# A dense graph network on one core: normalisation moved into attention's tail, APPNP's first body moved into the last product of layer 1

## The chip, the cores and the metric

The kernel runs on one core of a Trainium2 chip. The metric is device time in microseconds (us), as the median of three runs. In the text PE is TensorE, DVE is VectorE, ACT is ScalarE, POOL is GpSimd and SP is SyncE, whose queue issues the DMAs spoken of here.

## The reference

A graph of 6250 nodes with 96 features and 100,000 edges goes through four layers. Each layer takes `h = relu(layernorm(x))` and adds its result to x.

```python
h = jnp.maximum(_layernorm(x, axis=-1), 0.0)
x = x + _L0_gnn_ref(h, qW, kW, vW, src, dst)      # attention over the edges, itself h + res
h = jnp.maximum(_layernorm(x, axis=-1), 0.0)
x = x + _L1_gnn_ref(h, src, dst, W, b)            # softmax aggregation: (h + sum(a * m)) @ W + b
h = jnp.maximum(_layernorm(x, axis=-1), 0.0)
x = x + _L2_gnn_ref(h, edge_index)                # APPNP: ten times out = 0.9 * spmm(out) + 0.1 * h
h = jnp.maximum(_layernorm(x, axis=-1), 0.0)
x = x + _L3_gnn_ref(h, edge_index, W1, b1, W2, b2)  # two graph convolutions
...
# layer 1, per destination node and feature
m = relu(feat[src]) + EPS
ex = exp(m - seg_max[dst]);  denom = segment_sum(ex, dst)
msg = segment_sum(ex / denom[dst] * m, dst)
```

## The kernel before, in words

**Tiles and bodies.** The nodes lie in 49 tiles of 128. X (the running x), H (the norm's result) and T hold 49 x 96 floats per partition. Work on them goes in seven bodies of seven tiles (`BODIES` = `RING` = 7, `tiles_of(b)`), so one instruction on a body has 672 elements per partition.

**Attention.** A loop over pairs of tiles builds one-hot matrices from the edge list, gathers keys, values and queries with them on PE, and sums the weighted values. It also builds two dense count matrices in DRAM: `adjacency` (`c_d`), and its transpose `adjacency_t` (`t_d`), which SP writes through transposing DMAs. Each engine runs its own step function `lag` chunks behind the first; the last tile has five chunks (`last_chunks`) and is written out after the loop (`paired`). Attention's result per tile lies in R, whose first 49 tiles are T. Near the end DVE makes `most_all`, the largest count and degree, and `verdict` turns it through a PE transpose into a flag `fits`, which every engine loads before it branches into the dense layers. Nothing of the dense layers is ahead of that branch.

**Layer 1 (`softmax_dense`).** A prelude makes, for each body, X += T, the norm (`Norm.center`, `square`, `variance`, `deviation`, `scale`), exp, and the f16 operand U in high and low halves (384 columns and one of ones). DVE and ACT do it in a pipeline of turns. Then PE multiplies: for output body i and ring slot r it takes 7 x 7 matmuls of 385 columns from the slot into seven PSUM banks. A ring slot holds a block of counts for seven source tiles. Output body i needs U of all seven bodies, slot by slot, so the first output body consumes the prelude as it comes. After a body, ACT copies the low halves out, DVE adds and divides (`inv`, `dn`, T), PE applies the weight matrix in two parts of four and three tiles (`Folded`: transposes L449, products L465, in a bank of its own, called l), DVE adds to X, and the norm for the next layer follows, which ends with ACT writing Ua (`y` in the rows; u_ready). For bodies 0 to 5 these pieces lie between the matmuls of the next body; those of body 6 come after all (`folded.last`).

**APPNP.** Ten steps, each seven bodies of seven banks; bank r of a body takes 49 matmuls of 192 columns (one per source tile) from slot r, loaded from `adjacency_t`. The first bank of a step starts with 42 tiles and waits there for the last seven. ACT and DVE finish each bank (`rows`, `copies`), in loops on every engine. `degree_columns` stands ahead of it on DVE and ACT.

What sets the order is the code as written: each engine runs its queue in order, and semaphores join them.

## Time and profile before

| | us |
|---|---|
| Median of three runs (4059.42 to 4060.96) | 4060.95 |
| Profiled execution, its own time | 4059.11 |
| Its span in the profile | 4057.7 |
| PE busy | 3871.5 (95%) |
| DVE busy | 1833.1 (45%) |
| ACT busy | 1303.2 (32%) |
| POOL busy | 519.8 (13%) |

The profile is of one execution. Its time is 1.4 us above its span, which is what lies outside the span. An engine's share is over all stages; a change in one stage has to be read from that stage's rows.

### The profile page before, as it was taken

How to read it: one execution, taken by the hardware profiler on the slowest of the kernel's cores; microseconds unless marked ns; L12 is line 12 of the kernel's file. 1: busy time of each engine (PE TensorE's matmuls, PEld its weight loads, DVE VectorE, ACT ScalarE, POOL GpSimd, SP SyncE). 2: the span in 40 equal slices, each digit the busy share in tenths (PEclk: the TensorE clock that was granted, in tenths of full speed). 3: DMA queues.
4: the chain of work that ended last, by engine and by line, in shares of the span. 5: the costliest groups of instructions: out<-in, count | busy, mean ns of one | idle time of the engine just before them, and what ended most of it. 6: DMA issues, size and time to landing. Idle time of an engine off the chain costs nothing.

```text
span 4057.7 us, 123846 instructions
## 1 busy us (share of the span) xinstructions
PE 3871.5 (95%) x46211; PEld 3663.5 (90%) x46211; DVE 1833.1 (45%) x4350; ACT 1303.2 (32%) x3904; POOL 519.8 (13%) x708
## 2 busy tenths in 40 slices
PE   3779999999979998999999999999999998999998
PEld 2669999999956665999999999999999998999998
DVE  8989999999983224222222222222222222331221
ACT  1238878788871101222222222222222221111110
POOL 1005555555520000000000000000000000000000
PEclk9989999999989999999999999999999999999999
DMA  1029999999963332566656556656655665666674
GB/s 40 3 52 236 229 228 234 233 227 228 235 190 109 110 109 84 197 203 204 204 203 203 202 202 202 202 203 203 203 203 203 204 202 178 204 218 210 210 220 142
DMA packets 437963, 747.69 MB, mean 184 GB/s; under 512 B 197295, under 2 KB 330543, under 8 KB 437804
## 3 DMA queue, kind: packets, MB, share of 16 engines
q1 hardware_dynamic: 432808, 744.50, 60.9%
q8 instruction: 123, 2.02, 0.2%
q10 hardware_dynamic: 4996, 0.88, 0.1%
q14 instruction: 36, 0.29, 0.0%
HBM read 621.82 MB, written 83.32 MB: 174 GB/s over the span
## 4 chain that ended last, share of the span: by engine, by line
PE 91%; DVE 6%; ACT 1%; issue 1%; DMA 1%; ACTq 0%; SPq 0%; DVEq 0%
PE sum L1651 49%; PE sum L1344 19%; PE pk L1114 10%; PE pr L1137 7%; PE pq L1126 3%; PE pc L1150 2%; DVE onerank L759 2%; PE l L465 1%; DVE bt L731 1%; DVE prodb L748 1%; DVE vals L741 0%; PE l L449 0%; DMA X<-in_x_dram 0%; DVE sameb L736 0%; DVE kv L593 0%
## 5 line engine op out<-in xcount | busy, mean ns | idle before, releaser
L1651 PE MATMUL sum<-y,ring 128*128 128x192 f16 x12005 | 995.1, 247 | 4.0 <-ACT y L1500 4.0
L1651 PEld LDWEIGHTS sum<-y,ring 128*128 128x128 fp8e4 x12005 | 993.8, 98 | 4.6 <-issue 4.2
L1651 PE MATMUL sum<-u2b,ring 128*128 128x192 f16 x12005 | 993.0, 247 | 0.0
L1651 PEld LDWEIGHTS sum<-u2b,ring 128*128 128x128 fp8e4 x12005 | 992.1, 98 | 0.2
L1660 DVE TENSOR_TENSOR z<-lo,sum 128x96 f32<-128x96 f32 x441 | 112.3, 255 | 1006.7 <-ACT lo L1675 1006.1
L1114 PE MATMUL pk<-kv,hT 128*128 128x192 f16 x4900 | 487.1, 247 | 11.2 <-DVE hT L1008 9.6
L1344 PE MATMUL sum<-u,ring 128*128 128x385 f16 x2401 | 402.7, 328 | 22.2 <-ACT u L1468 22.2
L1114 PEld LDWEIGHTS pk<-kv,hT 128*128 128x128 f16 x4900 | 406.0, 99 | 18.2 <-DVE hT L1008 9.5
L1344 PEld LDWEIGHTS sum<-u,ring 128*128 128x128 fp8e4 x2401 | 235.7, 98 | 182.5 <-issue 24.6
L1675 ACT ACTIVATE lo<-sum 128x96 f32<-128x96 f32 x441 | 110.3, 250 | 668.5 <-PE sum L1651 668.5
L1137 PE MATMUL pr<-wv,hs_wide 128*128 128x101 f32 x2450 | 321.3, 278 | 1.2 <-POOL wv L1071 1.2
L1137 PEld LDWEIGHTS pr<-wv,hs_wide 128*128 128x128 f32 x2450 | 292.9, 192 | 1.5 <-POOL wv L1071 1.5
L1196 ACT ACTIVATE kvs<-pk 128x384 f32<-128x384 f32 x735 | 277.7, 441 | 25.6 <-PE pk L1114 21.6
L1071 POOL TENSOR_TENSOR wv<-kvs,wv 128x480 f32<-128x480 f32 x245 | 255.2, 1041 | 107.4 <-ACT wv L1176 107.4
L1066 POOL TENSOR_SCALAR sc<-sc,bound 128x20 f32<-128x20 f32 x245 | 188.7, 770 | 477.6 <-DVE sc L992 477.1
L1344 PE MATMUL sum<-u2b,ring 128*128 128x192 f16 x2401 | 203.0, 246 | 0.7 <-ACT u2b L1817 0.7
L1344 PE MATMUL sum<-y,ring 128*128 128x192 f16 x2401 | 202.2, 246 | 0.0
L1344 PEld LDWEIGHTS sum<-u2b,ring 128*128 128x128 fp8e4 x2401 | 199.1, 98 | 1.1 <-ACT u2b L1817 1.0
L1344 PEld LDWEIGHTS sum<-y,ring 128*128 128x128 fp8e4 x2401 | 199.0, 98 | 0.1
L1169 ACT ACTIVATE row<-pc 128x512 uint16<-128x512 f32 (+1 forms) x343 | 187.1, 549 | 1.0 <-PE pc L1150 0.2
L1186 ACT ACTIVATE hs_wide<-hs 128x640 f32<-128x640 bf16 x245 | 179.0, 731 | 0.0
L1663 DVE SCALAR_TENSOR_TENSOR uf<-z,col_g,H 128x96 f32<-128x96 f32 x441 | 140.6, 319 | 81.6 <-DVE z L1660 81.6
(237 smaller groups left out, 3412.6 us busy)
## 6 DMA issues: line engine op xcount, KB each, us to landing
ring<-adjacency_t SPq DMA_DIRECT2D x490, 800.0 KB, 4.3
ring<-adjacency SPq DMA_DIRECT2D x147, 896.0 KB, 4.8
rows<-slot_rows_d SPq DMA_DIRECT2D x249, 320.0 KB, 4.2
adjacency<-row SPq DMA_DIRECT2D x49, 800.0 KB, 4.3
adjacency_t<-col SPq DMA_DIRECT2D x49, 800.0 KB, 4.8
col<-row SPq DMA_TRANSPOSE x245, 4.5
out_dram<-X SPq DMA_DIRECT2D x6, 336.0 KB
ed<-in_dst_dram ACTq DMA_DIRECT2D x25, 18.0 KB, 1.7
```

Source lines behind the costliest of these rows:

```text
L1066: pool.tensor_scalar(sc[i][:], sc[i][:], k.bound[:, 0:1], k.bound[:, 1:2], ALU.min, ALU.max).then_inc(k.clipped.sem, 1)
L1071: pool.tensor_tensor(wv[i][:, :, 0:D].rearrange("p g (h d) -> p g h d", d=DH), kv[i][:, :, D:2 * D].rearrange("p g (h d) -> p g h d", d=DH ...
L1114: t = pe.matmul(pk[n][:, place:place + 2 * D], hT[i][:, 1 + m, g, :], k.kv[:, 2 * (g0 + g) + m, part, :], start=m == part == 0, stop=m == ...
L1126: t = pe.matmul(pq[i][:, g * D:(g + 1) * D], hT[i][:, 0, g, :], q2[b][:, part, :], start=part == 0, stop=part == 1)
L1137: t = pe.matmul(pr[:, 0:AV], hs_wide[e % HOMES][:, g, :], wv[i][:, g, :], start=g0 + g == 0, stop=g0 + g == GROUPS - 1)
L1169: a.activation(flat(row[b][:, g:g + count, :]), pc[u % 2][:, 0:count * P], ACT.Copy, accum_out=rowsum[:, bass.ds(X * (2 * UP) + u, 1)]).th ...
L1186: a.activation(flat(hs_wide[e % HOMES][:]), hs[e % 2][:].rearrange("p g a t -> p (g a t)"), ACT.Copy).then_inc(k.wide.sem, 1)
L1196: a.activation(flat(kv[i][:, 2 * n:2 * n + count, :]), pk[n][:, 0:count * 2 * D], ACT.Copy).then_inc(k.kv_out.sem, 1)
L1344: t = pe.matmul(self.ps[j][:, 0:self.cols], w[:, q, (j + odd) // 2, :, (j + odd) % 2], U[:, r * RING + q, 0:self.cols], start=r == q == 0, ...
L1651: m = pe.matmul(ps[r][:, 0:2 * D], w[:, t // 2, :, t % 2], n["this"][:, t, 0:2 * D], start=t == 0, stop=t == TILES - 1)
L1660: v.tensor_tensor(z[:, j, :], lo[:, j, :], ps[j][:, 0:D], ALU.add).then_inc(k.free.sem, 1)
L1663: v.scalar_tensor_tensor(uf[j][:], z[:, j, :], k.g[:, tile], flat(k.H[:, tile, :]), ALU.mult, ALU.add).then_inc(k.uf.sem, 1)
```

## The change

Four things are done.

1. In attention's tail, DVE does X += T and `center` for body 0 and ACT squares it (`first_norm`, at step `last_chunks + 1`); after the last operations on `most`, DVE does `variance` and `scale`, and ACT the root and the exp, all ahead of the verdict. SP loads ring slot 0 for layer 1 there, ahead of the last three transposes. For this the ring is seven buffers, of which the first lives from the start.
2. X += R of bodies 1 to 6 goes from DVE, where it stood in the prelude, to POOL, in one row after attention's last result. The column `odeg` is copied one step earlier on POOL, and one small operation of the verdict goes into the tail.
3. The prelude of layer 1 is written in another order: body 0's operand alone first, then body by body.
4. The last product of layer 1 goes straight on into APPNP's first body: six banks over 42 tiles, with the four pieces of body 6 between them, then the last seven tiles of these six banks, then bank 6. `adjacency_t` is loaded for it as the slots come free. DVE's chain of layer 1 is cut in two, four tiles and three. The loop over APPNP's steps is regrouped, with body 0 left out of the first step on PE and SP.

```diff
@@ sync_step
+        if chunks == last_chunks and c == SP_LAG:
+            Blocks.load(k, 0, 0)
@@ denominate / normalize
+        pool.tensor_copy(k.odeg[:, bass.ds(2 * X + b, 1)], sums[b][:, AV - 1:AV]).then_inc(k.degreed.sem, 1)
...
-        pool.tensor_copy(k.odeg[:, bass.ds(2 * X + b, 1)], sums[b][:, AV - 1:AV])
@@ paired
+            if meanwhile and c == last_chunks + 1:
+                meanwhile()
@@ vector (attention)
-        paired(v, vector_step)
+        paired(v, vector_step, meanwhile=first_norm)
...
+        norm.variance(0)
+        norm.scale(0)
+    def first_norm():
+        t = tiles_of(0)
+        v.wait_ge(k.normed.sem, k.normed.at((RING - 1) // 2, (RING - 1) % 2))
+        v.tensor_tensor(k.X[:, t, :], k.X[:, t, :], k.R[:, t, :], ALU.add).then_inc(k.added.sem, 1)
+        v.wait_ge(k.added.sem, k.added.at(1))
+        norm.center(0)
+    def gpsimd():
+        paired(pool, gpsimd_step)
+        pool.wait_ge(k.normed.sem, k.normed.at(PAIRS - 1, last_tiles - 1))
+        for b in range(1, BODIES):
+            t = tiles_of(b)
+            pool.tensor_tensor(k.X[:, t, :], k.X[:, t, :], k.R[:, t, :], ALU.add).then_inc(k.added2.sem, 1)
+    def scalar():
+        paired(a, scalar_step, meanwhile=lambda: norm.square(0))
+        norm.deviation(0)
+        a.wait_ge(k.ln_h.sem, k.ln_h.at(1))
+        a.activation(k.T[:, tiles_of(0), :], k.H[:, tiles_of(0), :], ACT.Exp).then_inc(k.exps.sem, 1)
@@ softmax_dense, vector
+            product(0)
+            remainders(0)
+            center(1)
+            norm.variance(1)
+            for b in range(1, BODIES):
+                if b + 1 < BODIES:
+                    center(b + 1)
+                norm.scale(b)
+                if b + 1 < BODIES:
+                    norm.variance(b + 1)
+                product(b)
+                remainders(b)
...
+                for h, (j0, j1) in enumerate(Folded.PARTS):
+                    for j in range(j0, j1):
...
+                    v.reciprocal(inverse, inverse).then_inc(k.inv.sem, 1)
@@ softmax_dense, tensor
-            blocks.tensor([k.lo2], folded)
+            for i in range(BODIES):
+                blocks.products(i, [k.lo2], folded)
+            first_products()
+            there = TILES - RING
+            pe.wait_ge(k.u_ready.sem, k.u_ready.at(there))
+            for r in range(RING - 1):
+                begin_panel(r)
+                for half in range(2):
+                    panel(r, range(half * there // 2, (half + 1) * there // 2))
+                    folded.piece(BODIES - 1, 2 * r + half - 2)
+            pe.wait_ge(k.u_ready.sem, k.u_ready.at(TILES))
+            for r in range(RING - 1):
+                panel(r, range(there, TILES))
+            begin_panel(RING - 1)
+            panel(RING - 1, range(TILES))
```

DVE's queue in attention's tail, before, from the last score sum on; `highest`, `filled` and `fits` are the verdict's.

```order
L992 TENSOR_REDUCE sc<-qk 128x20 [waits at_exped,at_scored]
L1044 RECIPROCAL rden<-rden 128x4 [waits at_denom]
L1242 CAST bits<-rowsum 128x343 [waits at_out_c]
L1244 TENSOR_REDUCE most<-odeg 128x1 [waits at_normed]
L1246 TENSOR_SCALAR bits<-bits 128x343 [waits most_s]
L1247 TENSOR_SCALAR most<-most 128x1
L1249 TENSOR_REDUCE most<-bits 128x1 [waits most_s]
L1251 TENSOR_TENSOR most_all<-most 128x1 [waits most_s]
L1271 TENSOR_REDUCE highest<-pf 1x1 [waits most_s,at_normed,most_ps,at_col_out1,at_col_out0]
L1273 TENSOR_SCALAR highest<-highest 1x1 [waits verdict]
```

The same place in the change:

```order
L1267 TENSOR_TENSOR X<-X,T 128x672 [waits at_normed]
L278 TENSOR_REDUCE col<-X 128x7 [waits added]
L280 TENSOR_SCALAR col<-col 128x7 [waits ln_sum]
L282 TENSOR_TENSOR H<-X,col 128x672 [waits ln_mean]
L1047 RECIPROCAL rden<-rden 128x4 [waits at_denom]
...
L1259 TENSOR_TENSOR most_all<-most 128x1 [waits most_s]
L292 TENSOR_REDUCE col<-T 128x7 [waits ln_sq]
L294 TENSOR_SCALAR col<-col 128x7 [waits ln_var]
L304 RECIPROCAL col<-col 128x7 [waits ln_std]
L306 SCALAR_TENSOR_TENSOR H<-H,col 128x672 [waits ln_rstd]
L1303 TENSOR_REDUCE highest<-pf 1x1 [waits most_s,at_normed,most_ps,at_col_out1,at_col_out0]
```

Four operations stand ahead of the last reciprocal of attention now, and four between `most_all` and the verdict's first.

ACT's queue from the last exp of attention to the first part of U, in the change (`wv` is that exp, `sums` attention's last sums):

```order
L1180 ACTIVATE wv<-sc,score_unit 128x5x4 [waits at_summed,at_clipped]
L287 ACTIVATE T<-H 128x672 [waits ln_cen]
L1207 ACTIVATE sums<-pr 128x101 [waits at_normed,at_summed]
L299 ACT_TABLE_LOAD
L299 ACTIVATE col<-col 128x7 [waits ln_vare]
L1282 ACT_TABLE_LOAD
L1282 ACTIVATE T<-H 128x672 [waits ln_h]
L1310 TENSOR_LOAD fits [waits most_s,at_normed,verdict,at_col_out1,at_col_out0]
```

The square stands ahead of the copy of attention's last sums; root, exp and their two table loads stand ahead of the verdict. Before, they came after it.

PE's queue at the end of layer 1, before, from the last slot's last banks on (l is the bank of the weight matrix's pieces):

```order
L1344 MATMUL sum_6<-u,ring 128x385 x7
L449 MATMUL l<-ident,T 96x128 [waits lin_out,agg]
L449 MATMUL l<-ident,T 96x128 x3
L465 MATMUL l<-wl,aT 128x96 [waits lin_copied]
L465 MATMUL l<-wl,aT 128x96 x3
L449 MATMUL l<-ident,T 96x128 [waits lin_out,agg]
L449 MATMUL l<-ident,T 96x128 x2
L465 MATMUL l<-wl,aT 128x96 [waits lin_copied]
L465 MATMUL l<-wl,aT 128x96 x2
```

The same place in the change:

```order
L1558 MATMUL sum<-y,ring 128x192 [waits ring0,free,u_ready]
L1558 MATMUL sum<-y,ring 128x192 x41
L1558 MATMUL sum<-y,ring 128x192 [waits ring1,free]
L1558 MATMUL sum<-y,ring 128x192 x41
L449 MATMUL l<-ident,T 96x128 [waits lin_out,agg]
L449 MATMUL l<-ident,T 96x128 x3
L1558 MATMUL sum<-y,ring 128x192 [waits ring2,free]
L1558 MATMUL sum<-y,ring 128x192 x20
L465 MATMUL l<-wl,aT 128x96 [waits lin_copied]
L465 MATMUL l<-wl,aT 128x96 x3
L1558 MATMUL sum<-y,ring 128x192 x21
L449 MATMUL l<-ident,T 96x128 [waits lin_out,agg]
```

84 matmuls of APPNP's first body are ahead of the first piece, 21 between each two pieces, and 105 more follow the last one ahead of the wait for the last seven tiles.

## Rows read from the trace of the kernel before

**Rows 1.** The page: chain that ended last, shares of the span by line.

```profile
PE sum L1651 49%; PE sum L1344 19%; PE pk L1114 10%; PE pr L1137 7%; PE pq L1126 3%; PE pc L1150 2%; DVE onerank L759 2%; PE l L465 1%; DVE bt L731 1%; DVE prodb L748 1%; DVE vals L741 0%; PE l L449 0%; DMA X<-in_x_dram 0%; DVE sameb L736 0%; DVE kv L593 0%
```

**Rows 2.** Chain in order of time, longest pieces: start us, us, what.

```profile
1183.97 74.78 PE sum L1344 x441
...
1285.32 32.41 PE sum L1344 x196
...
1623.06 1809.40 PE sum L1651 x21910
```

**Rows 3.** Chain, around the verdict.

```profile
1157.78 3.33 DMA adjacency_t<-col
...
1162.54 0.16 DVE fits L1277
...
1163.46 0.95 DVE X L1413
```

**Rows 4.** Chain, from layer 1's last product to APPNP.

```profile
1580.19 16.22 PE sum L1344 x98
...
1599.03 4.36 DVE inv L1434
...
1605.20 0.87 DVE T L1440
...
1613.70 0.47 DVE X L1391
```

**Rows 5.** Timeline of the tail: start us, us, engine, line, operation, [idle before <-releaser].

```profile
1151.63 0.65 DVE L992 TENSOR_REDUCE sc<-qk 128x20 f32<-128x480 f32 x1
...
1152.50 0.35 POOL L1066 TENSOR_SCALAR sc<-sc,bound 128x20 f32<-128x20 f32 x1 [0.46 <-DVE sc L992]
...
1155.73 0.26 ACT L1203 ACTIVATE sums<-pr 128x101 f32<-128x101 f32 x1 [2.53 <-PE pr L1137]
...
1157.46 0.34 POOL L1089 TENSOR_TENSOR T<-sums,rden 128x96 f32<-128x96 f32 x1
```

**Rows 6.** Timeline of the kernel's start, DVE beside POOL.

```profile
23.58 1.60 POOL L212 TENSOR_TENSOR X<-X,H 128x672 f32<-128x672 f32 x1 [21.17 <-DVE H L306]
24.29 0.91 DVE L294 TENSOR_SCALAR col<-col 128x7 f32<-128x7 f32 x1
...
49.86 1.60 POOL L212 TENSOR_TENSOR X<-X,H 128x672 f32<-128x672 f32 x1 [1.87 <-DVE H L306]
49.87 1.90 DVE L510 TENSOR_TENSOR wq_squares<-wq 96x288 f32<-96x288 f32 x1
```

**Rows 7.** DVE's groups, 1152 to 1240: count | busy us, mean ns | idle before.

```profile
L306 DVE SCALAR_TENSOR_TENSOR H<-H,col 128x672 f32<-128x672 f32 x7 | 6.0, 858 | 0.2
...
L294 DVE TENSOR_SCALAR col<-col 128x7 f32<-128x7 f32 x7 | 1.2, 172 | 0.2
```

**Rows 8.** Timeline, ACT in the prelude of layer 1.

```profile
1171.04 0.76 ACT L287 ACTIVATE T<-H 128x672 f32<-128x672 f32 x1 [2.35 <-DVE H L282]
...
1171.83 1.28 ACT L1476 ACT_TABLE_LOAD   x1
...
1173.12 0.76 ACT L1476 ACTIVATE T<-H 128x672 f32<-128x672 f32 x1
```

**Rows 9.** Timeline, ACT's copy of a body's seventh bank (layer 1's first, APPNP's first).

```profile
1242.64 0.33 ACT L1489 ACTIVATE lo<-sum 128x192 f32<-128x192 f32 x1 [0.83 <-PE sum L1344]
...
1649.75 0.25 ACT L1675 ACTIVATE lo<-sum 128x96 f32<-128x96 f32 x1 [1.52 <-PE sum L1651]
```

**Rows 10.** Chain, two pieces of the weight matrix within a later body.

```profile
1553.62 0.44 PE l L449 x4
...
1562.16 0.86 PE l L465 x8
```

**Rows 11.** Windows: stretch, length, PE, PEld, DVE, ACT, POOL busy, PEclk, DMA share, GB/s.

```profile
1606.00:1616.00 10.00, 7.89 (x37) 6.64 (x38) 2.92 (x7) 1.08 (x2) 0.00 (x0) 0.50 0.01 6
...
1170.00:1175.00 5.00, 0.00 (x0) 0.00 (x0) 4.79 (x10) 3.88 (x5) 0.00 (x0) 0.50 1.09 386
```

More of the change, by code:

```diff
@@ L1352, in products, with sync @@
                 folded.piece(i - 1, r)
-    def sync(self, ended=None):
+    def sync(self, ended=None, early=0):
         n = len(self.U) * BODIES
         for i in range(n):
-            self.loads(i)
+            self.loads(i, 0 if i else early)
             if ended and i >= 2:
@@ L1421, in vector @@
                 v.wait_ge(k.agg.sem, k.agg.at(i))
-                for j in range(RING):
-                    t = RING * i + j
-                    v.wait_ge(k.low.sem, k.low.at(t + 1))
-                    v.tensor_tensor(dn[:, j, :, :], lo[:, j, :, :], halves(ps[j])[:, :, 0, :], ALU.add).then_inc(k.sums.sem, 1)
-                    v.tensor_scalar(k.ideg[:, t:t + 1], ps[j][:, cols - 1:cols], UNIT, None, ALU.mult).then_inc(k.free.sem, 1)
-                tiles = tiles_of(i)
-                v.wait_ge(k.free.sem, k.free.at(RING * i + RING))
@@ L1638, in loads @@
             k.settle(sp)
[L1639 removed]
+            sp.dma_start(k.ring[r][:, 0:WIDE], k.t_d[RING * n["body"] + r, :, :]).then_inc(k.ring_in[r].sem, 16)
     def products(n):
@@ L1683, in numbers, with bodies @@
     def numbers(eng):
-        def bodies(step, U, Un):
+        def bodies(step, U, Un, first=0):
             if eng is pe:
@@ L1688, in bodies @@
                 k.settle(pe)
-            with eng.Fori(0, BODIES) as i:
+            with eng.Fori(first, BODIES) as i:
                 yield {"step": step, "body": i, "at": step * BODIES + i, "this": U, "next": Un}
+        yield from bodies(0, Ua, Ub, 1 if eng in (pe, sp) else 0)
         with eng.Fori(0, last // 2) as s:
-            yield from bodies(2 * s, Ua, Ub)
             yield from bodies(2 * s + 1, Ub, Ua)
-        yield from bodies(last - 1, Ua, Ub)
+            yield from bodies(2 * s + 2, Ua, Ub)
     def last_numbers():
@@ L1846, in dense_layers @@
     with ExitStack() as ctx:
-        k.ring = k.buf(ctx, "ring", [P, RING, SLOT], U8)
+        k.ring += [k.buf(ctx, f"ring_{r}", [P, SLOT], U8) for r in range(1, RING)]
         Y = k.buf(ctx, "y1", [P, TILES, D], F32)
         Ua = Y[:].bitcast(F16)
-        with ExitStack() as banks:
-            softmax_dense(k, [k.bank(banks, f"sum1_{j}") for j in range(RING)], k.bank(banks, "l1"), Y, Ua)
-        appnp_and_convolutions(k, ctx, [k.bank(ctx, f"sum2_{j}") for j in range(RING)], k.bank(ctx, "l3"), Ua, out)
+        ps, bank = [k.bank(ctx, f"sum_{j}") for j in range(RING)], k.bank(ctx, "l")
+        softmax_dense(k, ps, bank, Y, Ua)
+        appnp_and_convolutions(k, ctx, ps, bank, Ua, out)
 class Edges:
```

180 lines of the change are left out of this document (101 added, 79 removed).

## The prediction, as it was put on record

> **What bounds the kernel now.** The page's chain first: it is PE almost throughout, most of it APPNP's matmuls [rows 1]. So the change can only win where PE stands. The chain in order of time shows two such places: PE ends attention just ahead of ACT's copy at 1155.73 [rows 5] and starts layer 1 at 1183.97 [rows 2], and it ends layer 1's last product at 1580.19 + 16.22 = 1596.41 [rows 4] and starts APPNP for good at 1623.06 [rows 2], after 42 early matmuls. Then I read both places in the chain and the timeline, for what ends each wait. A matmul of 385 columns costs 32.41 / 196 = 0.1654 us, a body's slot of 49 costs 8.10, one of 192 columns 1809.40 / 21910 = 0.0826, a bank of 49 costs 4.05 [rows 2].
>
> **First place, the tail, without contention.** Before, the verdict's last operation ends at 1162.70, DVE's first of layer 1 starts at 1163.46 [rows 3], and the prelude lasts until 1183.97. After, body 0's norm and exp are there. What is left is three DVE operations on a body (product, two remainders, 0.86 each, as L306 [rows 7]) and one ACT copy (0.76, as the exp [rows 8]). With one small verdict operation less (0.17 [rows 7]), PE would start at 1163.3 + 3 x 0.87 + 0.9 = 1166.8.
>
> **What POOL takes back.** DVE stands beside POOL's X += H on a body, 1.60 us [rows 6]: a tensor_scalar that takes 0.17 alone [rows 7] took 0.91, until POOL ended, and a small tensor_tensor started at 49.87 ended at 51.77, just after POOL's 51.46. So DVE's operations with two SBUF inputs, and its tensor_scalar, wait for POOL's current operation. The change puts six such POOL operations, 9.6 us, right behind attention's last result, beside the DVE operations that lead to the verdict.
>
> When do they start? The last score sum ends at 1152.28; DVE's X += T takes until 1153.15, and POOL's clip, before at 1152.50, waits for it: 0.7 late, and exp, weighting and sums with it. DVE's reduction ends at 1154.0, its tensor_scalar waits for POOL's weighting, the centred H is there at 1156.0 (0.86 each), ACT's square at 1156.8. The copy of the last sums stands behind it: 1156.8 for 1155.73 [rows 5]. POOL's last result, before at 1157.80 [rows 5], comes at 1158.85, and its six additions start there.
>
> If both engines take turns, the maximum on DVE comes at 1160.7 (if single-column tensor_scalars don't need the port) or 1162.4 (if they do); then the variance (reduction 0.86, tensor_scalar behind an addition), root and reciprocal 0.5, scale behind an addition: 1164.9 or 1166.6. The verdict's maximum 0.3, comparison, and `fits` behind one or two more: 1166.65 or 1170.1, for 1162.70. From there 0.75 to the branch, and three DVE operations, two or none of them behind an addition: PE starts at 1173.25 or 1174.35. I take 1173.8. Each addition can block once, so both ends lie close. If DVE got no turn until POOL is through (1168.5), what needs the port after the maximum follows from there: 1176.
>
> Behind this cover the rest of the tail costs nothing. The exp's two table loads (1.28 each [rows 8]) and the exp end at 1165.7 or 1167.4, ahead of `fits`. SP's load of slot 0 (0.92 MB, 2.4 us at 386 GB/s [rows 11]) stands ahead of three transposes and the stores that end at 1161.11 [rows 3]; even 2.4 us late, 1163.5, PE's transpose of the maximum is done before DVE gets to its result. Without POOL's contention those 2.4 us would be the loss.
>
> The Trainium skill, SBUF — State Buffer, § Who interferes with whom, says that the pair is an exclusive lock, held by whichever starts first for the whole instruction, by a DVE operation with two SBUF inputs against a POOL operation that reads SBUF, and that a tensor_reduce never contends. By this rule, the trace agrees with it (0.91 for 0.17).
>
> **The prelude, body by body.** PE wants a body's U every 8.10 us. In the new order the engines hand each body back and forth: from the second remainder of body b-1, DVE centres b+1 (1.95), ACT squares (0.76), loads a table (1.28), takes the exp (0.76) and its copy (0.77) of b, loads the root's table (1.28), takes the root (0.2, half of it beside the next) and the second copy (0.75), and DVE takes the second remainder (0.86); with gaps of 0.02 and the root's wait 8.68. Body 1 has no head start: its U comes 12.3 after PE's start (centre 1.95, square and table 2.1, root; centre of 2 and square 2.4; table, exp, copy, table, root, copy 5.0; remainder and copy 1.7, less the 0.9 between remainder and PE's start). PE's first slot ends at 8.1 + 1.95 for the low clock: the first body of before ended at 1242.62 [rows 9], 58.65 after its start for 343 x 0.1654 = 56.7. So PE waits 2.3 for body 1 and 0.58 for each of 2 to 5; body 5 is ready at 12.3 + 4 x 8.68 = 47.0, body 6 needs two things less and is in time. The first body ends 47.0 + 2 x 8.10 = 63.2 after PE's start: 1237.0, for 1242.62. **Gain 5.6.** X += T of six bodies off DVE (0.86 each) helps only in that DVE isn't the longer of the two. The later slots are 0.92 MB each, landed at 2.4 us apart, ahead of 8.10.
>
> The Trainium skill, ScalarE: Activation LUTs, § What ACT_TABLE_LOAD costs, has every switch at about 2.66 us, with a drain of 1.38 beside the load. Here the square ends at 1171.80, the load starts at 1171.83 and the exp at 1173.12: 1.28 and no drain [rows 8]. By the page a body would take 8.68 + 2.76 = 11.4 and this place would lose about 8 us; by the row it gains 5.6.
>
> **Second place: into APPNP.** Slots and U are there: each slot is free 8.1 us after the one before, long ago, and Ua of bodies 0 to 5 since the piece of body 5. PE runs on at 1596.43 with 84 matmuls, 6.9 us, to 1603.4. DVE's chain: four tiles are summed at 1593.8 (three banks of 1.16 ahead of PE's end, and 0.9 for ACT's copy and DVE's sum) and cost 4/7 of a chain in which the reciprocal is 4.36 and five others 0.87 [rows 4, 7]: to 1599.1; then three tiles' sums (1.3) and 3/7: T at 1604.7 for 1606.07 [rows 4]. Banks 4 to 6 are freed at 1599.5, 1599.9 and 1600.4; in the six bodies where PE wants them again, it does so 4 x 1.16, 5 x 1.16 and 6 x 1.16 after the body's end, 1601.0 and later: covered by 1.5 us. PE waits 1.3 for T. Pieces at full clock are 0.44 and 0.86 for four tiles [rows 10], three quarters for three. With the 21 matmuls (1.73) that stand between them: transposes to 1605.3, 21 to 1607.0, products to 1608.0, DVE 0.56, 21 to 1609.7, transposes 1610.1, 21 to 1611.8, products to 1612.6, DVE's last addition to 1613.1, for 1614.17 [rows 4]. From there to PE's start on the last seven tiles it is 1623.06 - 1614.17 = 8.89 as before: 1622.0. PE has 105 matmuls, 8.7, until 1621.2, waits 0.8, and takes 42 + 49 in 7.5: APPNP's first body ends at 1629.5. Before, 1649.7 [rows 9]: 301 x 0.0826 = 24.9 after 1623.06, and 1.8 left over, which the new order doesn't repeat if the clock stays up. **Gain 20.2.** Rows and loads of the next body start as banks end and have 4.05 each for 2.6 of work on ACT and DVE, so the crowd of six early banks is gone within the next body.
>
> **Sum.** 5.6 + 20.2 = 25.8 off the profiled execution's 4059.11. The median lies 1.84 above it: 4060.95 - 25.8 = **4035 us**.
>
> **Rivals.**
> *Low clock across the second place.* Before, the granted clock was 0.50 from 1606 to 1616 although PE worked there [rows 11], after 9.7 us of idling. If the 1.3 us of waiting brings it about, at half speed the four pieces take 2.3 longer and the three times 21 matmuls between them at most 5.2. I take 6 of these 7.5, since the fall needn't cover all: gain 14, total 20: 4041. For it: small matmuls and waits. Against: PE is busy nine tenths of the place. 0.17.
> *No turns for DVE in the tail*, or a body cycle longer by half a microsecond: the first place gives 2 or nothing: 4038 to 4041. 0.16.
> *POOL hardly in the way*: the operations that stand beside its additions don't need the port, as the trace shows only two kinds [rows 6]. Then PE starts at 1166.8 plus up to 2.4 for the slot's load, gain 5 to 7 more: 4029. Against: both kinds are the ones used here. 0.10.
> *Slower, by layer 1's banks.* The split chain sits ahead of the sums of banks 4 to 6. If it takes longer than worked out by more than the cover of 1.5 us, PE stalls at bank 4 of each of six bodies. To turn 25.8 us into a loss of 8, it must stall 5.6 a body: the four tiles' part would take 12.4 us instead of 5.3. 0.04.
> *The change doesn't do what it says in the second place*: APPNP's early banks wait for a slot or a bank, so that PE idles as before. Against: slots come free 8.1 us apart. 5.6 us of gain, 4055. 0.04.
> *Table switches stand still for longer than the load*, say another 1.28 each, now that ACT's chain is the one that PE waits for. Body 1 would come 3 x 1.28 later, each further body 2.56: the first place loses 8, the total gain is 12, 4049. The exp right behind its load speaks against it [rows 8]. 0.01.
> The forecast has 0.48.
>
> **Range.** 4029 to 4043 takes in the forecast and the first three rivals, 0.91, with 2 us for the estimates in them. A measurement of this kernel tells a difference from 0.2%, 8.1 us. Faster than that: all cases but two, 0.92; within it (the second place not doing what it says) 0.04; slower 0.04.
>
> **What would show it.** POOL has six operations of about 1.6 from 1158.9 on, and DVE's tensor_scalar and two-input ones between `most_all` and the verdict last until one of them ends. `fits` ends 4 to 7 us later than before, PE starts layer 1 near 1174, waits 2 to 3 us at its second slot and about 0.6 at the next four. T of body 6 comes 8.3 after the last product's end, PE idles under 3 us from there to the end of APPNP's first body, at a clock of 1.00, and from then on everything is as before. The prediction is wrong if POOL and DVE run side by side, if the clock falls in the second place, or if a later body of layer 1 is longer than 343 x 0.1654 + 2.3 for its four pieces = 59.0.

## The result, and the profile after

Four runs of the changed kernel gave a median of 4033.39 us (4032.60 to 4033.83), four of the kernel before 4060.62 (4059.42 to 4060.96): 27.2 us less, a ratio of 0.9934 with a 95% interval of 0.9923 to 0.9946. 4035 had been forecast. The profiled execution has a span of 4032.1 us.

In the page after, the chain by line still is TensorE's [rows 1], and a line of APPNP's early matmuls (L1558) is new in it.

The first place, in the timeline after. These rows answer to [rows 5] (last score sum), [rows 3] (`fits`) and [rows 2] (TensorE's start at 1183.97):

```profile
1152.43 0.65 DVE L995 TENSOR_REDUCE sc<-qk 128x20 f32<-128x480 f32 x1
...
1160.08 10.62 POOL L1276 TENSOR_TENSOR X<-X,T 128x672 f32<-128x672 f32 x6
...
1160.36 0.15 DVE L1257 TENSOR_SCALAR most<-most 128x1 f32<-128x1 f32 x1
...
1163.78 1.74 DVE L306 SCALAR_TENSOR_TENSOR H<-H,col 128x672 f32<-128x672 f32 x1
...
1165.92 1.06 DVE L1307 TENSOR_TENSOR fits<-filled,highest 1x1 int32<-1x1 f32 x1
...
1167.75 1.50 DVE L1496 SCALAR_TENSOR_TENSOR y<-H,T 128x672 f32<-128x672 f32 x1 [0.77 <-DVE fits L1307]
...
1169.17 2.25 DVE L1502 TENSOR_TENSOR T<-T,u 128x672 f32<-128x672 f32 x1
1171.35 0.85 DVE L1504 TENSOR_TENSOR y<-y,u 128x672 f32<-128x672 f32 x1
...
1173.09 9.63 PE L1379 MATMUL sum<-u,ring 128*128 128x385 f16 x49 [8.14 <-ACT u L1521]
1185.39 34.23 PE L1379 MATMUL sum<-u,ring 128*128 128x385 f16 x196 [2.67 <-ACT u L1521]
1219.82 30.43 PE L1379 MATMUL sum<-u,ring 128*128 128x385 f16 x183 [0.19 <-ACT u L1521]
```

While GpSimd adds (1160.08 to 1170.70), H takes 1.74 us for its 0.86 [rows 7], T takes 2.25, and `fits`, one element, 1.06. The single-column tensor_scalar at 1160.36 takes 0.15 in the same stretch, and the row at 1171.35, right after GpSimd is through, 0.85. TensorE starts at 1173.09 and ends its first body at 1219.82 + 2 x 8.10 = 1236.02, for 1242.62 before.

One thing in this profile was in no forecast. TensorE's last ten matmuls of attention stand ahead of the copy of the last sums, and so ahead of GpSimd's additions. In the timeline after:

```profile
1155.56 2.46 PE L1141 MATMUL pr<-wv,hs_wide 128*128 128x101 f32 x10 [1.31 <-POOL wv L1074]
```

and in that of place1_only (below), which has the same tail:

```profile
1155.49 1.36 PE L1141 MATMUL pr<-wv,hs_wide 128*128 128x101 f32 x10 [1.31 <-POOL wv L1074]
```

The wait ahead of them is the same 1.31 us (0.88 before). From 1156 to 1158 the granted clock is 0.50 in the one and 1.00 in the other.

The second place, in the chain after (start us, us, what). It answers to [rows 4]:

```profile
1597.32 0.47 DVE T L1475
...
1597.83 0.64 PE l L449 x4
1598.47 1.73 PE sum L1558 x21
1600.20 0.89 PE l L465 x8
...
1605.60 0.47 DVE X L1428
...
1622.55 2.48 PE sum L1731 x30
```

and two rows of its windows, after:

```profile
1600.00:1616.00 16.00, 15.35 (x181) 15.12 (x179) 8.09 (x16) 3.62 (x8) 0.00 (x0) 1.00 0.01 3
...
1616.00:1632.00 16.00, 16.00 (x197) 16.00 (x195) 6.05 (x23) 4.34 (x18) 0.00 (x0) 1.00 0.95 382
```

Layer 1's last product ends at 1590.03, T is there 7.8 us later and TensorE is through with APPNP's first body 32.5 us later, at 1622.55; before it was 53.3 us. The granted clock is 1.00 (2.4 GHz) in the whole place, where before it was 0.50 [rows 11].

### The profile page after: what moved, and what is told of

It reads as the page before. It is cut to its first block, busy times and chain, and to the rows that moved or that the text cites. A ratio compares the mean times of both kernels' runs of the same rounds, so it can differ in the third digit from the quotient of the medians.

```text
span 4032.1 us, 123897 instructions
## 1 busy us (share of the span) xinstructions
PE 3868.6 (96%) x46211; PEld 3661.2 (91%) x46211; DVE 1835.6 (46%) x4386; ACT 1303.0 (32%) x3904; POOL 526.1 (13%) x714
## 3 DMA queue, kind: packets, MB, share of 16 engines
q8 instruction: 126, 2.06, 0.2%
## 4 chain that ended last, share of the span: by engine, by line
PE 90%; DVE 6%; ACT 1%; issue 1%; DMA 1%; SPq 0%; ACTq 0%; DVEq 0%
PE sum L1731 48%; PE sum L1379 18%; PE pk L1118 10%; PE pr L1141 7%; PE pq L1130 3%; PE pc L1154 2%; DVE onerank L759 2%; PE l L465 1%; DVE bt L731 1%; DVE prodb L748 1%; DVE vals L741 0%; PE l L449 0%; DMA X<-in_x_dram 0%; PE sum L1558 0%; DVE sameb L736 0%
## 5 line engine op out<-in xcount | busy, mean ns | idle before, releaser
L1731 PE MATMUL sum<-y,ring 128*128 128x192 f16 x11662 | 962.9, 246 | 0.0
L1731 PEld LDWEIGHTS sum<-y,ring 128*128 128x128 fp8e4 x11662 | 962.2, 98 | 0.0
L1379 PEld LDWEIGHTS sum<-u,ring 128*128 128x128 fp8e4 x2401 | 236.0, 98 | 172.7 <-issue 11.9
L1379 PE MATMUL sum<-y,ring 128*128 128x192 f16 x2401 | 202.2, 246 | 0.0
L1379 PEld LDWEIGHTS sum<-y,ring 128*128 128x128 fp8e4 x2401 | 199.0, 98 | 0.1
```

What stands on the lines that cost most here:

```text
L1379: t = pe.matmul(self.ps[j][:, 0:self.cols], w[:, q, (j + odd) // 2, :, (j + odd) % 2], U[:, r * RING + q, 0:self.cols], start=r == q == 0, ...
L1731: m = pe.matmul(ps[r][:, 0:2 * D], w[:, t // 2, :, t % 2], n["this"][:, t, 0:2 * D], start=t == 0, stop=t == TILES - 1)
```

## The experiments

Eleven kernels ran, in three groups that each had runs of the kernel before beside them. The table gives medians; "gain" is that of the kernel before in the same group less this one. The kernel before itself moved by up to 1.6 us between groups (4060.62, 4060.01, 4059.22, 4059.01), so a difference of under 1.5 us between two gains is read from stages of the trace and not from the table. Seven are the changed kernel with one edit; place1_only and place2_only undo one half of it, and combined and combined_slot have several edits.

| kernel | median us | before beside it | gain |
|---|---|---|---|
| the changed kernel | 4033.39 | 4060.62 | 27.2 |
| place1_only | 4053.21 | 4060.01 | 6.8 |
| place2_only | 4038.63 | 4060.01 | 21.4 |
| pieces_first | 4046.05 | 4060.01 | 14.0 |
| no_split | 4035.36 | 4060.01 | 24.7 |
| late_slot | 4032.06 | 4059.22 | 27.2 |
| dve_adds | 4035.15 | 4059.22 | 24.1 |
| paced_adds | 4033.39 | 4059.22 | 25.8 |
| dev_last | 4029.97 | 4059.22 | 29.3 |
| squares_early | 4018.67 | 4059.01 | 40.3 |
| combined | 4013.77 | 4059.01 | 45.2 |
| combined_slot | 4012.76 | 4059.01 | 46.3 |

One more thing has to be known before stages are compared. Attention's last score sum starts at 1152.43 in the changed kernel and at 1151.63 before [rows 5]. The difference grows steadily through attention's loop. In the timeline of DVE, the same two score sums of the loop, one from its middle and one from its end, for the changed kernel:

```profile
595.32 0.64 DVE L995 TENSOR_REDUCE sc<-qk 128x20 f32<-128x480 f32 x1
...
1137.03 0.64 DVE L995 TENSOR_REDUCE sc<-qk 128x20 f32<-128x480 f32 x1
```

and for place2_only, which has attention as before:

```profile
595.10 0.64 DVE L993 TENSOR_REDUCE sc<-qk 128x20 f32<-128x480 f32 x1
...
1136.20 0.64 DVE L993 TENSOR_REDUCE sc<-qk 128x20 f32<-128x480 f32 x1
```

541.71 us lie between them for 541.10; the ten others with the changed tail have 541.7 to 542.0, and the kernel before 541.11. That is the second half of the loop only. From the tenth score sum (322.04 after, 322.19 before) to the one at 1137.03 it is 814.99 for 814.04, so the loop is 1.0 us longer. The only edit within the loop is GpSimd's copy of the degrees, which now stands between the denominator and the wait for DVE's inverse. That this copy is what costs the 1.0 us was not tried by itself. In the eleven kernels with the changed tail the last sum starts anywhere from 1151.67 to 1152.90, so in the first place I count from that start: TensorE's first matmul of layer 1 stands 20.66 behind it in the changed kernel.

In four kernels that leave the first place untouched (place1_only, pieces_first, no_split, squares_early) it stands 19.72 behind it. There the last ten matmuls of attention take 1.36 and not 2.46, and GpSimd's additions start 6.71 behind the last score sum and not 7.65. So 0.94 of the 20.66 us are the low clock ahead of the additions, in the one execution that was profiled.

### The two places apart

place1_only undoes the second place, place2_only the first (tail, verdict and prelude as before).

```diff
-            for i in range(BODIES):
-                blocks.products(i, [k.lo2], folded)
-            first_products()
+            blocks.tensor([k.lo2], folded)
```

> The second half of the change is undone (APPNP's first body runs after layer 1's last product, DVE's chain is whole), the tail and the prelude stay as changed. Theory, that the two places add up and share no resource: layer 1's first body still ends at 1236.0 and its last product at 1590.1, and the time is the time before less 6.4, so 4054.2 (4053 to 4055.5). Rival, that the places lean on each other (the earlier prelude is worth less, or more, without the second): a gain of 4 or less, or 9 or more, so over 4056.5 or under 4052.

> The tail, the verdict and the prelude are as before, only the second place is changed. Theory of two places that add up: layer 1 as before (its first body ends at about 1242.6, its last product at about 1596.4), and the end of APPNP's first body 32.5 after that last product, so the time before less 20.8, 4039.8 (4038.8 to 4041). Rival: a part of the 20.8 comes from the first place, then the first body ends more than 34 after the last product and the time is over 4041.5.

The diff shows the main lines of place1_only; place2_only takes back the whole of the tail and the prelude. Measured: 6.8 and 21.4, ratios 0.9984 (0.9974 to 0.9993) and 0.9950 (0.9933 to 0.9966). Together 28.2, for 27.2 of both: the places add up. place1_only's 4053.21 lies in its range, place2_only's 4038.63 is 0.2 under its own. In place2_only, TensorE's rows show the prelude of before (start at 1184.00), and the chain shows APPNP's first body 32.5 us behind the last product, which ends at 1596.4, as in the changed kernel:

```profile
1628.87 11.14 PE sum L1700 x135
```

### The order of the second place

pieces_first puts the four pieces of the last linear ahead of APPNP's panels in TensorE's queue.

```diff
             there = TILES - RING
+            folded.last()
...
                 for half in range(2):
                     panel(r, range(half * there // 2, (half + 1) * there // 2))
-                    folded.piece(BODIES - 1, 2 * r + half - 2)
```

> The four pieces of the last linear (two of transposes, two of products) stand in TensorE's queue before APPNP's first panels and not between them; nothing else is changed. Theory, that the 84 matmuls of two panels and a half fill waits for DVE and ACT that are there anyway: with the pieces first, TensorE stands idle while T is made and copied, the panels begin only behind the last piece, and APPNP's first body ends later by about what those panels take that no longer fit, at most the 10.7 that 126 matmuls of 7.1 us for 84 give, less what still fits under the norm behind the last piece; I take 3 to 10.7, with 4033.4 + 7 = 4040 as middle. Rival, that the interleaving is worth nothing because all of the panels fit under DVE's chain behind the last piece: same within 1 us.

no_split lets DVE work on seven tiles at once.

```diff
-                for h, (j0, j1) in enumerate(Folded.PARTS):
+                for h, (j0, j1) in enumerate(((0, RING),)):
```

> DVE's chain of layer 1 works on all seven tiles at once again, as before the change; APPNP's first body still begins in layer 1's last product. Theory, that the split lets the first four tiles' transposes and copy run beside the chain of the last three: T is finished earlier without the split (one chain and not two), the transposes and copy of the first four tiles come later, net the first body ends later by 1 to 3, time about 4035.3. Rival, that the ready semaphore is raised only after both parts and so the split costs its six more instructions: the unsplit one is faster by 1 to 2, about 4032.

pieces_first lost 12.7 us by the medians and 13.2 by the gains, more than the 10.7 I had given as the most. TensorE's rows in its timeline:

```profile
1597.34 1.09 PE L449 MATMUL l<-ident,T 128*96 128x128 f32 x4 [7.80 <-DVE T L1475]
1599.11 2.02 PE L465 MATMUL l<-wl,aT 97*128 97x96 f32 x8 [0.68 <-ACT aT L458]
1601.87 0.84 PE L449 MATMUL l<-ident,T 128*96 128x128 f32 x3 [0.74 <-DVE X L1428]
```

It waits 7.80 for T, then 0.68 and 0.74, and its pieces take twice the 0.64 and 0.89 of the changed kernel: the granted clock was 0.50 from 1592 to 1608. All 343 matmuls of the body come behind the last piece, 30.20 us from 1604.89, and the body ends 45.6 us after layer 1's last product and not 32.5. I had counted 126 matmuls that no longer fit in front. The two chains give the 13.1 us in three parts. The 84 matmuls that ran under the wait for T now run behind it: 84 x 0.0826 = 6.9. The pieces take 5.6 us for 2.5 and the 343 matmuls 30.2 for 28.3, at the low clock: 4.9, which I had left out. TensorE waits 1.95 between the pieces for ACT and DVE, where the changed kernel waits 0.65 for the last copy: 1.3. The 3 x 21 matmuls between the pieces cover only those waits; their own time is on the chain in either order.

no_split lost 2.0 (2.6 by the gains). T comes 9.7 us after the last product (ended at 1588.34, T at 1598.02), 1.9 later than with the split. My median of 4035.3 was met, but not by its theory, which had T earlier without the split and nothing of the clock. The body ends 35.95 after the product, 3.4 later. The other 1.5 stands in TensorE's rows of the timeline:

```profile
1598.07 1.09 PE L449 MATMUL l<-ident,T 128*96 128x128 f32 x4 [2.79 <-DVE T L1475]
1598.95 3.00 PE L1558 MATMUL sum<-y,ring 128*128 128x192 f16 x21
```

and in its windows:

```profile
1596.00:1600.00 4.00, 1.93 (x11) 1.79 (x12) 2.05 (x4) 0.59 (x1) 0.00 (x0) 0.72 0.00 0
```

After a wait of 2.79 the four transposes take 1.09 for 0.64 and the 21 matmuls behind them 2.79 in the chain for 1.73, and the granted clock is 0.72 in that window. In the changed kernel the wait there is 0.87 and the clock stays at 1.00. So the rival of a low clock in the second place was real: in the profile without the split it is there. Counted from the last score sum, no_split's first place is 0.9 shorter than that of the changed kernel (no low clock in attention's end), so 3.4 less 0.9 stands beside the 2.6.

### Who lengthens DVE's operations, and what that costs

dve_adds takes the additions of bodies 1 to 6 off GpSimd; paced_adds leaves two behind attention and hands out the other four, one in each body.

```diff
+            pool = k.pool
+            for b in range(3, BODIES):
+                t = tiles_of(b)
+                pool.wait_ge(k.res2.sem, k.res2.at(b - 2))
+                pool.tensor_tensor(k.X[:, t, :], k.X[:, t, :], k.T[:, t, :], ALU.add).then_inc(k.added2.sem, 1)
```

> The six additions of bodies 1 to 6 are on DVE again, one before each body's mean, and GpSimd does none. Theory, that GpSimd's additions lengthened DVE's operations between 1160 and 1171 by taking the port: H L306 is back from 1.74 to 0.86, fits from 1.06 to about 0.1 or 0.2, y from 1.50 to 0.86, T from 2.25 to 0.86, so TensorE's first body begins near 1169.8 and not 1173.1; then body 1 comes 0.9 later behind its own addition. Layer 1's first body ends 1 to 3 earlier, and the time is about 4031.5. Rival, that the lengthening is not due to GpSimd (a wait inside the instruction): the same durations stay, and the time is 0.9 or more slower for the additions on DVE.

> GpSimd adds bodies 1 and 2 behind attention as now, and each of bodies 3 to 6 only when the remainders of body b - 3 are taken (one addition of 1.6 to 1.8 in each body). Theory, that only the overlap of the additions with the first body's chain costs: additions end near 1163.6, H, fits, y and T of the first body take 0.9 or less each, TensorE's first matmul comes near 1169.9, a gain of 3.1 kept until the end, since the later additions fall where DVE waits for ACT: 4030.3. Rival, that the additions cost the same wherever they stand: each later body is lengthened by 0.7, the gain is under 1.

DVE's and TensorE's rows in the timeline of dve_adds:

```profile
1161.70 0.86 DVE L306 SCALAR_TENSOR_TENSOR H<-H,col 128x672 f32<-128x672 f32 x1
1166.08 0.15 DVE L1303 TENSOR_TENSOR fits<-filled,highest 1x1 int32<-1x1 f32 x1
1166.99 0.94 DVE L1493 SCALAR_TENSOR_TENSOR y<-H,T 128x672 f32<-128x672 f32 x1 [0.77 <-DVE fits L1303]
1167.84 0.85 DVE L1499 TENSOR_TENSOR T<-T,u 128x672 f32<-128x672 f32 x1
...
1170.52 10.12 PE L1375 MATMUL sum<-u,ring 128*128 128x385 f16 x49 [5.07 <-ACT u L1518]
1184.61 18.02 PE L1375 MATMUL sum<-u,ring 128*128 128x385 f16 x98 [3.97 <-ACT u L1518]
...
1213.11 8.27 PE L1375 MATMUL sum<-u,ring 128*128 128x385 f16 x49 [1.23 <-ACT u L1518]
1222.62 27.62 PE L1375 MATMUL sum<-u,ring 128*128 128x385 f16 x166 [1.24 <-ACT u L1518]
```

Every length is back (0.86, 0.15, 0.94, 0.85), and TensorE starts 17.62 behind the last score sum and not 20.66. Of these 3.0 us, 0.94 are the low clock in the changed kernel's profile; against the four kernels at 19.72 it is 2.1, and that GpSimd's additions cost this much of the start is shown. It isn't more because the last transfer of adjacency_t holds the verdict here: it lands 11.9 behind the last score sum, and `highest` follows it by 0.8. But the body cycle is now 1222.62 - 1213.11 = 9.5, for 8.60 in the changed kernel. TensorE waits 3.97 for body 1 and 1.24 at the last two; the last wait ends 2.3 later than in the changed kernel, counted from the last score sum. My 4031.5 had priced one addition of 0.9 on the path, where each body has one.

paced_adds starts TensorE at 17.55, and then shows:

```profile
1169.28 10.90 PE L1379 MATMUL sum<-u,ring 128*128 128x385 f16 x49 [5.07 <-ACT u L1521]
1182.32 8.27 PE L1379 MATMUL sum<-u,ring 128*128 128x385 f16 x49 [2.15 <-ACT u L1521]
1191.65 8.27 PE L1379 MATMUL sum<-u,ring 128*128 128x385 f16 x49 [1.06 <-ACT u L1521]
```

The cycle is 9.35, longer by 0.75. Of 3.1 us at the start 0.1 is left at TensorE's last wait (67.25 behind the last score sum for 67.39), and the median is the same 4033.39. Against the four kernels at 19.72, whose last wait ends 66.45 behind the sum, it is 0.8 worse. My theory fell and its rival held: spread over the bodies of this chain, which goes back and forth between DVE and ACT, each addition costs nearly what it costs on DVE (0.75 for 0.9).

The Trainium skill, SBUF — State Buffer, § Who interferes with whom, has the DVE operations with two SBUF inputs and the GpSimd ones that read SBUF exclude each other for a whole instruction and leaves the reduction alone. These runs agree: 0.86 for 1.74 with the additions gone, and a variance reduction of 0.84 at 1161.62 in the middle of them.

### Slot 0 of the ring

```diff
-        if chunks == last_chunks and c == SP_LAG:
-            Blocks.load(k, 0, 0)
...
-        scalar(), vector(), scalar_sums(), tensor(), blocks.sync(early=1), first_loads()
+        scalar(), vector(), scalar_sums(), tensor(), blocks.sync(), first_loads()
```

> Slot 0 of the ring is loaded behind the verdict again, and not in attention's tail. Theory, that the early load only fills a place where nothing waits for it: the last adjacency_t transfer lands about 3 earlier (near 1161.1 and not 1164.3), but the verdict's last product is held by DVE's H anyway and moves by less than 0.4; slot 0 then lands about 4.6 after its issue, near 1172.6, just before TensorE's first operand at 1173.1. Time within 0.5 of the changed kernel. Rival one, that the three crowded transfers of the tail hold up the verdict: faster by 1 or more. Rival two, that seven loads issued together bring slot 0 later than 1173.1: TensorE's first matmul waits for the ring, slower by 1 to 4.

The gain is the same 27.2 (its median is 1.3 under that of the changed kernel, and the kernel before in its group is 1.4 lower too). The last transfer starts at 1158.91 instead of 1161.00 and lands 9.55 behind the last score sum, for 11.89, and nothing comes of it. DVE's rows of late_slot show why:

```profile
1163.65 1.73 DVE L306 SCALAR_TENSOR_TENSOR H<-H,col 128x672 f32<-128x672 f32 x1
1165.31 0.27 DVE L1301 TENSOR_REDUCE highest<-pf 1x1 f32<-1x128 f32 x1
...
1165.80 1.07 DVE L1305 TENSOR_TENSOR fits<-filled,highest 1x1 int32<-1x1 f32 x1
```

The verdict's maximum stands behind H on DVE, which GpSimd holds up, whether the transfer lands at 1162.2 or at 1164.3. The early load is worth nothing and costs nothing, as long as that cover lasts. In dve_adds, where it doesn't, TensorE starts 17.62 behind the last sum, held by this transfer.

### ACT's root behind both low halves

```diff
-                if 1 <= b < BODIES - 1:
-                    norm.deviation(b + 1)
...
                 if b == 0:
                     norm.square(1)
+                if b < BODIES - 1:
                     norm.deviation(b + 1)
```

> ACT takes the root for body b + 1 (and loads the table of the root) behind both low halves of body b, not between its first and its second copy. Theory from the rows: TensorE waits 2.67 at 1185.4 for body 1's last ACT copy, which stands behind that table load of 1.28; from there on it has hardly any wait (196 matmuls in 34.2). So body 1's copy comes 1.3 to 1.5 earlier, and nothing is gained behind it: 4033.4 - 1.4 = 4032.0. Rival, that the body cycle of 8.6 on ACT sets the pace of all the bodies: with the cycle at 8.1 or less a gain of 3 or more, 4030 or less.

3.4 us less than the changed kernel by the medians, 2.1 by the gains; TensorE's stage gives 3.5. TensorE's rows in the timeline, and ACT's loads of the root's table:

```profile
1173.02 9.91 PE L1379 MATMUL sum<-u,ring 128*128 128x385 f16 x49 [8.38 <-ACT u L1519]
...
1184.00 1.28 ACT L299 ACT_TABLE_LOAD   x1
1184.04 64.98 PE L1379 MATMUL sum<-u,ring 128*128 128x385 f16 x392 [1.11 <-ACT u L1519]
...
1191.63 1.28 ACT L299 ACT_TABLE_LOAD   x1
```

Body 1's copy comes 1.35 earlier (1.5 counted from the last score sum), as expected, but that is not all. ACT's cycle is 1191.63 - 1184.00 = 7.63, for 8.60, so that now TensorE's 8.10 sets the pace: four times 0.5 more. So the rival that I had put beside my theory held. I had read the unbroken row of 196 matmuls in 34.23 us (after, at 1185.39) as TensorE working without a wait. 196 x 0.1654 is 32.4. A window of the changed kernel:

```profile
1186.00:1190.00 4.00, 4.00 (x16) 1.95 (x14) 3.00 (x6) 3.51 (x4) 0.00 (x0) 0.57 0.26 93
```

The slower matmuls filled the time in which others of these kernels show a wait of 0.33 in each body (place1_only, pieces_first and late_slot, whose TensorE rows stand 8.60 apart). The low clock cost nothing there, because ACT's chain ended last either way: from body 1's copy to the last wait it is 34.43 us in the changed kernel and 34.43 in place1_only, whose clock stays at 1.00.

### The squares of the weights

Both traces show TensorE waiting 10.8 us in APPNP's last step for a product of DVE's that nothing keeps from being made earlier. In the timeline before:

```profile
3443.26 0.74 PE L1595 MATMUL l<-w_squares,ones 97*128 97x96 f32 x2 [10.81 <-DVE w_squares L1590]
```

```diff
     def last_rows():
+        unit.squares()
...
-            if b == 0:
-                unit.squares()
```

> DVE squares the weights of the first convolution before the rows of APPNP's last step, and no longer behind body 0's norm; otherwise the changed kernel. Theory from the row PE l <- DVE w_squares 10.8 of the trace after (it stands in the trace of before too): TensorE waits there for nothing but this product, and what it does next has been ready for long, so the time falls by the whole wait, to 4033.4 - 10.8 = 4022.6 (4021.5 to 4024), and a little more if the granted clock after the wait was below full. Rival: behind the wait TensorE meets DVE's and ACT's rows of body 0 anyway (free banks, the lo copies), then less than half of it is gained, 4028 or more.

4018.67, 14.7 less than the changed kernel by the medians (13.1 by the gains). The changed kernel, TensorE's wait in the timeline and a stretch of the windows:

```profile
3416.11 0.74 PE L1676 MATMUL l<-w_squares,ones 97*128 97x96 f32 x2 [10.82 <-DVE w_squares L1671]
```

```profile
3410.00:3420.00 10.00, 3.89 (x23) 3.70 (x24) 4.02 (x8) 2.50 (x4) 0.00 (x0) 0.50 0.01 2
```

and squares_early, the same stretch:

```profile
3410.00:3420.00 10.00, 10.00 (x124) 10.00 (x122) 5.43 (x12) 2.28 (x7) 0.00 (x0) 1.00 0.68 226
```

The wait is gone, and so is the half clock behind it: the next 2058 matmuls take 169.79 us for 172.30. The stage from the end of the panels before to layer 3 is 13.8 shorter: 10.8 of wait and 3.0 of clock. The time is 2.8 under the range I had given: I had the second part as "a little more". The 0.9 between 13.8 and 14.7 is the first place, whose profile has no low clock in attention's end here.

### Together

combined has dev_last, paced_adds and squares_early; combined_slot has slot 0's load behind attention's last transfer as well.

```diff
-        if chunks == last_chunks and c == SP_LAG:
-            Blocks.load(k, 0, 0)
...
     vector(), gpsimd(), paired(pe, tensor_step), scalar(), paired(sp, sync_step, SP_LAG)
+    Blocks.load(k, 0, 0)
```

> Three edits on the changed kernel: ACT's root behind both low halves, GpSimd's additions two behind attention and four paced, the squares of the weights early. The first alone made ACT's cycle 7.64 against TensorE's 8.10, so that there is 0.46 of room in each body; the paced additions alone lengthened the cycle from 8.61 to 9.35 but began TensorE 3.1 earlier. Theory that the two fit together (the 0.75 of an addition goes mostly into that room, since it delays a mean that is not what ACT waits for): body 1's copy 2.1 earlier than with the late root alone and TensorE without a wait behind it, so 4030.0 - 2.1 - 10.8 = 4017.1 (4015.5 to 4018.5). Rival, that the additions cost 0.7 in each later body here too: the cycle is 8.3 to 8.4, of the 2.1 about 1 is left or nothing, 4018.3 to 4019.5.

> As the one before, and slot 0 of the ring is loaded behind the last adjacency_t transfer instead of ahead of the last two transfers of attention. Theory: the last transfer lands about 3 earlier relative to attention's last sum (9.6 behind it and not 11.9 to 12.0), and with DVE's H no longer held up by GpSimd the verdict then comes 1.5 earlier; slot 0 lands before the verdict's branch, and TensorE's first matmul is 15.9 behind the last sum instead of 17.5. All later work moves with it: the combined time less 1.6, 4015.5. Rival one: body 1 and TensorE's own work bind, and of 1.6 nothing is left (within 0.5 of the combined one). Rival two: slot 0's transfer, issued 7 to 10 later, collides with the other six and TensorE starts later than 17.5: slower by 0.5 to 2.

combined: 4013.77, ratio to before 0.9887 (0.9870 to 0.9903). TensorE's rows:

```profile
1171.03 10.67 PE L1379 MATMUL sum<-u,ring 128*128 128x385 f16 x49 [5.07 <-ACT u L1519]
1182.80 64.98 PE L1379 MATMUL sum<-u,ring 128*128 128x385 f16 x392 [1.09 <-ACT u L1519]
```

No wait behind body 1, with an addition in each body: the cycle (GpSimd's additions stand 8.06 apart) now has the room for it. Body 1's copy is 1.5 earlier than in dev_last, counted from the last score sum, of 2.1 expected. The time is 3.3 under the expected 4017.1 and 1.7 under its range; squares_early alone had been 3.9 better than expected.

combined_slot: 4012.76 (4012.30 to 4013.69), ratio 0.9886 (0.9869 to 0.9902). Its chain around the verdict:

```profile
1158.22 4.38 DMA adjacency_t<-col
...
1163.85 0.16 DVE fits L1306
...
1164.77 0.94 DVE y L1495
```

The last transfer takes 4.38 for 3.33, with slot 0 behind it; TensorE starts 16.31 behind the last score sum, for 18.21 in combined, so the first place gives 1.9. By the medians it is 1.0, and the ranges of the two kernels' runs overlap: shown in the stage, not in the time. It is the fastest of all and beats the changed kernel by 20.6 us by the medians, the kernel before by 46.3.

## Why the prediction was right

**The sum.** Forecast 5.6 and 20.2; the stages of the profile show 6.6 and 20.8, and the two kernels with one place each 6.8 and 21.4. 6.6 + 20.8 = 27.4 stands beside the 27.2 measured; 4035 was 1.6 too high. That each part comes so near is in part luck, as the first place shows.

**The first place.** The mechanism held as put: GpSimd's additions lengthen DVE's two-input operations and its tensor_scalar on seven columns (0.77 at 1162.49, for 0.17 [rows 7]), not the reductions. Of the two ends for single-column tensor_scalars the lower one is right (0.15 and 0.14 in the middle of the additions). TensorE's start at 1173.1 lies just under the forecast's 1173.25 to 1174.35. That is nearer than the working deserves. The last score sum came 0.8 later than I had it: attention's loop, where I had costed the moved copy of the degrees at nothing, is 1.0 longer. And 0.94 is the low clock of attention's last ten matmuls, which I hadn't thought of; I had looked for a low clock in the second place only. Against these two stands a chain from the last score sum to the start that I had worked out too long: 21.6 at its lower end (1173.25 - 1151.63) for the 19.72 of the four kernels without the low clock. That DVE wins turns is in the trace after: H ends at 1165.52 and `fits` at 1166.98, with GpSimd adding until 1170.70. The rival that GpSimd is hardly in the way is refuted by dve_adds, by 2.1 to 3.0 us. The prediction set 0.91 for 0.17 beside the rule on two-input operations, but that row is a tensor_scalar's; the pair of rows that bears the rule out is H's 1.74 for 0.86. The prelude behind the start took 62.9 for 63.2, with 2.67 of wait for body 1 (2.3 forecast) and a cycle of 8.60 (8.68). Of the 1.0 us between 5.6 and 6.6, 0.7 is the start and 0.3 the stretch behind it.

**The additions off DVE.** I had valued them only as keeping DVE from being the longer of the two engines. dve_adds shows more: with an addition before each body's mean the cycle is 9.5 for 8.60, since DVE's work is in one chain with ACT's.

**Slot 0.** Costed at nothing for its cover, DVE's H behind GpSimd; late_slot shows just that. The transfer itself landed 3.2 later, of which 0.8 is the later last score sum: 2.4, as I had it. And that these 2.4 us would be the loss without GpSimd's additions is borne out by dve_adds (17.62 for a forecast of 1166.8 + 2.4, 17.6 behind the last score sum) and by combined_slot, which gets 1.9 of them back.

**Second place.** T came 7.8 after the last product, 8.3 forecast (by the terms that the prediction writes down, 1599.1 + 1.3 + 3/7 of 8.71, it would be 7.7; I had added half a microsecond without naming it); TensorE waited 0.87 for it (1.3) and 0.65 for the last copy (0.8); the first body ended 32.5 after the product, 33.1 forecast. no_split and pieces_first show that both parts of the edit are needed, the split for 3.4 us and the matmuls ahead of and between the pieces for 13.1, of which 1.5 and 4.9 are a low clock that they kept away. The six bodies before were not held up by the split chain (354.0 us from the end of the first to the last product, for 353.8 before), so the slower rival has nothing to show.

**Low clock.** I gave it 0.17, and in the second place it did not come. It would have come from small causes: with a wait of 2.79 in the same spot it did. Where it did come, in attention's end, it had no term in the sum.

**Table switches.** ACT's load is 1.28 and the next operation starts 0.01 or 0.02 behind it in all these traces (1191.63 above is one; the chain of dev_last has the exp's load at 1178.54 and the exp at 1179.83). The Trainium skill, ScalarE: Activation LUTs, § What ACT_TABLE_LOAD costs, has 1.38 more for a drain at each switch. No run here shows it, and the measurement decides: with it a cycle of two switches could not be 7.63.

**What was left out.** The forecast treated the new order of ACT as given. Two further waits lay in reach and in sight of the rows: ACT's root ahead of the second copy, 3.5 us, and the squares in APPNP's last step, which the profile before shows as the same wait of 10.8.

## What to carry to other kernels

When one engine hands work back and forth with another, find the cycle of that chain from the distance of like rows, not from how unbroken the third engine's row looks: a lower granted clock can fill a wait. An operation moved to another engine to relieve the chain still costs what it blocks there: on DVE the six additions cost 0.9 in each body, on GpSimd all at once 2.1 at the start, spread over the bodies 0.75 in each, and nothing in the cycle only once ACT's root had moved and left room. And list the single long waits of the bounding engine in the whole program before working on any place: one line moved on DVE brought half as much as the whole change.

## What the hardware showed that I had not expected

- The granted clock of TensorE stayed at 1.00 over waits of 0.87 and 0.65 with dense work around them, and fell to half for some us behind a wait of 2.79 in the same spot (no_split), of 7.80 (pieces_first) and of 10.82 (APPNP's last step), where it cost 3.0 us on top of the wait. In front of body 1 it fell behind a wait of 2.67 (after, 0.57 from 1186 to 1190), one of 2.53 (no_split, 0.50 from 1186 to 1188) and one of 2.44 (squares_early, 0.50 from 1186 to 1188), and did not behind 2.33 (place1_only), 2.14 (late_slot) and 1.11 (dev_last).
- The same wait can go either way. In all eleven kernels with the changed tail TensorE waits 1.31 ahead of attention's last ten matmuls. In three profiles the clock fell behind it and they took 2.46 (after), 2.25 (dev_last) and 2.06 (late_slot); in the other eight they took 1.36.
- A `fits` of one element took anything from 0.15 to 1.07 us, by where it fell in GpSimd's current addition (0.51 in place1_only, 0.25 in pieces_first, 0.18 in no_split; in all three it ended 13.61 behind the last score sum), while tensor_scalars on one column kept their 0.14 to 0.17.
- Attention's last transfer, of adjacency_t, took 3.33 before, the same with slot 0's load issued ahead of it, and 4.38 with that load issued right behind it (combined_slot).
